# A wait of GpSimd between groups of gathers, moved from ahead of a group's second gather to ahead of its last

## What is computed

```python
e = jnp.stack([tbl_0[ids[:, 0]], tbl_1[ids[:, 1]], ..., tbl_25[ids[:, 25]]], axis=1)    # 512 x 26 x 128
combined = jnp.concatenate([dense[:, None, :], e], axis=1)                             # 512 x 27 x 128
interactions = jnp.einsum('bfd,bgd->bfg', combined, combined)
iu, ju = jnp.triu_indices(27, k=1)
z = jnp.concatenate([dense, interactions[:, iu, ju]], axis=1)
h = jnp.concatenate([z, dense], axis=1)                                                # 512 x 607
h = jnp.maximum(h @ W_top1 + b_top1, 0.0)                                              # 607 -> 512
h = jnp.maximum(h @ W_top2 + b_top2, 0.0)                                              # 512 -> 256
y = h @ W_top3                                                                         # 256 -> 1
```

## Time and profile before

| | us |
|---|---|
| median of 3 runs (145.75 to 149.02) | 146.39 |
| the profiled execution | 147.18 |
| its span, first to last instruction | 145.4 |
| POOL busy / PE busy in the span | 80.0 / 103.3 |
| ACT busy / DVE busy | 72.3 / 75.0 |
| mean granted TensorE clock (share of full) | 0.881 |

### The profile page before, as it was taken

How to read it: one execution, slowest core, us unless ns; L and a number is a source line. 1 busy time by engine, 2 the same in 40 slices (tenths; PEclk the granted TensorE clock), 3 DMA queues, 4 the chain that set the end, 5 groups by cost and what they waited for, 6 DMA issues and landing times.

```text
span 145.4 us, 2762 instructions
## 1 busy us (share of the span) xinstructions
PE 103.3 (71%) x1052; PEld 93.8 (65%) x1052; DVE 75.0 (52%) x181; ACT 72.3 (50%) x179; POOL 80.0 (55%) x89
## 2 busy tenths in 40 slices
PE   0677659990349961899399974989939493694993
PEld 0366458980139950887399963979929392592992
DVE  3499993579200628289068008960662993057000
ACT  6798494821112999635169632041694232158111
POOL 2677644627556677685667776776777675000000
PEclk9999955599556999789999999599999999689599
DMA  4844798562822211121211221221121122000000
GB/s 164 230 125 117 196 305 251 134 180 70 316 71 58 54 43 54 52 52 41 52 43 54 60 60 36 59 54 52 43 54 54 42 53 56 2 5 0 0 0 1
DMA packets 6291, 11.96 MB, mean 82 GB/s; under 512 B 2683, under 2 KB 3295, under 8 KB 6150
## 3 DMA queue, kind: packets, MB, share of 16 engines
q0 software_dynamic: 2624, 5.38, 14.0%
q1 hardware_dynamic: 3509, 6.15, 13.9%
q10 hardware_dynamic: 144, 0.26, 0.5%
HBM read 10.65 MB, written 0.00 MB: 73 GB/s over the span
## 4 chain that ended last, share of the span: by engine, by line
DMA 46%; POOL 27%; issue 13%; PE 9%; DVE 3%; ACT 1%; POOLq 0%
DMA rows<-in_tbl_dram,ids_i 44%; POOL rows L419 27%; PE ps L740 4%; DVE z L586 3%; PE ps L702 2%; DMA ids_i<-in_ids_dram 2%; PE ps L752 1%; PE ps L647 1%; DVE z L587 0%; PE ps L762 0%; PE ps L681 0%; ACT emb_t L485 0%; ACT y L521 0%; DVE h_t L614 0%; POOLq L206 0%
## 5 line engine op out<-in xcount | busy, mean ns | idle before, releaser
L419 POOL DMA_INDIRECT rows<-in_tbl_dram,ids_i x82 | 79.2, 966 | 41.7 <-DMA rows<-in_tbl_dram,ids_i 21.0
L552 DVE TENSOR_SCALAR hot<-ps,row_no 125x256 fp32r<-125x256 f32 x73 | 29.8, 475 | 18.3 <-PE ps L634 18.2
L494 ACT COPY z<-ps 32x80 f32<-32x80 f32 (+2 forms) x80 | 25.8, 323 | 13.8 <-PE ps L702 12.9
L664 PE MATMUL ps<-hot,tab_hi 125*128 125x256 f32 x88 | 27.7, 340 | 4.4 <-ACT emb_t L464 4.3
L681 PE MATMUL ps<-ident,rows 128*128 128x128 f32 x82 | 15.1, 304 | 21.2 <-DMA rows<-in_tbl_dram,ids_i 17.7
L667 PE MATMUL ps<-hot,tab_lo 125*128 125x256 f32 x88 | 26.7, 329 | 1.7 <-DVE tab_lo L540 1.7
L681 PEld LDWEIGHTS ps<-ident,rows 128*128 128x128 f32 x82 | 9.8, 152 | 24.3 <-DMA rows<-in_tbl_dram,ids_i 19.7
L485 ACT COPY emb_t<-ps 128x512 f32<-128x512 f32 (+2 forms) x22 | 12.7, 579 | 24.7 <-PE ps L681 24.5
L664 PEld LDWEIGHTS ps<-hot,tab_hi 125*128 125x128 f32 x88 | 20.7, 235 | 5.4 <-ACT emb_t L464 4.8
L667 PEld LDWEIGHTS ps<-hot,tab_lo 125*128 125x128 f32 x88 | 20.8, 236 | 2.2 <-DVE tab_lo L540 2.2
L586 DVE COPY z<-ps 32x80 f32<-32x80 f32 (+2 forms) x42 | 13.1, 313 | 14.5 <-PE ps L702 13.9
(11 more groups left out here) (48 smaller groups left out, 92.2 us busy)
## 6 DMA issues: line engine op xcount, KB each, us to landing
tab<-in_tbl_dram SPq DMA_DIRECT2D x6, 448.0 KB
rows<-in_tbl_dram,ids_i POOLq DMA_INDIRECT x82, 2.5
w_fold<-w_pair SPq DMA_DIRECT2D x1, 1024.0 KB
w<-in_W_top_dram SPq DMA_DIRECT2D x1, 512.0 KB, 6.8
tab<-in_tbl_dram SPq DMA_DIRECT2D x6, 52.0 KB
x_rows<-in_r_dense_features_dram ACTq DMA_DIRECT2D x1, 256.0 KB, 2.9
w_x<-in_W_top_dram SPq DMA_DIRECT2D x1, 256.0 KB, 4.2
h_t<-in_W_top_dram SPq DMA_DIRECT2D x1, 256.0 KB, 4.7
```

The source lines that it names most:

```text
L419: pool.indirect_dma_start(out=rows[:, t % 2, gathered.index(f), :], out_offset=None, in_=tables[f - 1], in_offset=bass.IndirectOffsetOnAxi ...
L494: last = nc.scalar.copy(dst, src)
L552: nc.vector.tensor_scalar(hot[0:RP, k % OHB], ps[0:RP, IDV[h] + n % 2, 0:HB], row_no[0:RP, c:c + 1], None, ALU.is_equal).then_inc(hot_dve, 1)
L664: nc.tensor.matmul(bank, tab_hi[0:RP, n, c], one_hot, start=c == 0, stop=False)
```

## The change

The wait keeps its condition and its semaphore. Only the gather ahead of which it stands is another: no longer the second (n = 1) but the last of the group (n = len(fetched) - 1).

```diff
                     for n, f in enumerate(fetched):
-                        if n == 1 and g:
+                        if n == len(fetched) - 1 and g:
                             pool.wait_ge(rows_in[t][g - 1], 16 * sum(a > 0 for a in features(groups_of(t)[g - 1])))
-                        elif n == 1 and t:
+                        elif n == len(fetched) - 1 and t:
                             pool.wait_ge(rows_in[t - 1][NG - 1], 16 * len(features(groups_of(t - 1)[NG - 1])))
                         pool.indirect_dma_start(
```

## The result

The changed kernel takes 141.01 us in the median of 4 runs (140.90 to 141.15), the kernel before 147.17 (145.75 to 149.02): 0.965 of it, 95% interval 0.962 to 0.969. The ratios leave out runs more than 1.5% above the fastest of their kernel, so 0.965 stands for 5.1 us and the two medians lie 6.2 apart. On another chip the ratio was 0.963 (0.958 to 0.968). The forecast was 140.8. The profiled execution took 141.03 us and its span 139.1, against 147.18 and 145.4.

A forecast was written before the change was run, and what follows sets the result against it. The prediction took POOL's issue of 82 gathers, held back by waits for landings, as the bound. Gains of 2.0 us early and 3.6 steady, 5.6 in all, took 146.39 to 140.8 us; range 136.5 to 143.8.

The forecast's parts named there:

- Steady part: From 49.1 us on: 13 moved waits are hidden, each leaving only POOL's pause; gain 3.6 us.
- The cover: From 49.1 us on: extra gathers issued meanwhile hide the landing, 3.2 us at longest against 3.75; failing, gain 0.
- case 5: Rival: waits from 49.1 us on cost nothing beyond the landing, only the earlier stretch gains; 144.4 us, chance 0.02.
- Early part: Up to 49.1 us: gathers issued earlier gain 2.0 us, low bound 1.6, high bound 7.0.
- Step two: Tile 0, group 4: the awaited gather lands at 31.5 as before; the group's last goes at 31.8, before 34.28.
- case 2: Rival: landings follow issues before 49.1 us too, gain there up to 7.0; 135.5 to 139 us, chance 0.13.
- Step three: Tile 0, group 5: the awaited gather takes 4.0 us, landing at 35.8; the second gather goes at 36.1, before 37.04.
- Step four: Tile 1, group 0: the awaited gather lands at 40.5 under the copy; the third goes at 40.8, gain 1.7 us.
- PE follows: Tiles 1 to 3: PE keeps up; the gather still decides at tile 3's group 5, by 3.5 us.
- Tail: From 123.94 us to the end: 21.5 us without gathers, unchanged.
- the forecast's own sign: At the kernel's end: a tail not 21.5 us long would show the forecast wrong.
- Slower, by gathers that take turns from the loads: Rival: extra gathers in flight at 20 to 24 us delay tables and weights; about 149.1 us or more, chance 0.04.

The follow-up runs named there:

- the first pair: Profiled executions of the kernel before and the changed kernel, from the main measurement: 147.18 and 141.03 us, spans 145.4 and 139.1.
- the second: Traces of the same two kernels run again without edit: medians 147.11 us before and 141.49 us changed, ratio 0.963.

## Why the prediction was right, point by point

**What bounds the kernel:** right. The gathers set the end, and still do.

**Steady part, forecast 3.6 us, measured 4.2** in the first pair and 5.3 in the second. All 13 moved waits are hidden: between 50 and 122 only four are left, those of group 5 in tiles 1 to 3 and one that costs 0.30, which is the pause. Idle time accounts for 3.9 of the 4.2, and gathers on which POOL itself was busy for longer than 0.94 (1.07, 1.19 and 1.41 before, 1.07 and 1.36 after) for 0.3. The 1.40 at 68.09 became 0.54, and another group 5 got 1.19: these vary from trace to trace, as the forecast left open. The cover held, with little to spare in groups of three: the longest landing was 3.5 against 3.75. (The forecast took 3.2 for the longest before; the chain has one of 3.34, issued at 64.49, still under 3.75.)

By the estimate of 2.15 us to landing from the Trainium skill (DMA: Bandwidth & Descriptors, Anatomy of one DMA) nothing would have been left to gain here. The traces had 2.5 and the gain came, so case 5 was rightly small.

**Early part, forecast 2.0 us, measured 0.9 in the first pair, 1.9 between the means.** That 2.0 and 1.9 agree is luck. The forecast put the start of the steady part at 47.1 (49.1 less 2.0), and all three traces with the new place have it at 48.2 to 48.5, over 1 us later. The mean comes out right because before starts it at 50.2 on average, while the forecast had only the trace with 49.1. Two steps were wrong, and they cancelled in part. Step two said that the gather of 23.5 would land at 31.5 as before, since the queue decides; it landed at 29.4, after 5.94, near its time of before. Group 4's last gather then went at 29.69 and not at 31.8, which the forecast had called the sign of case 2; case 2 did not come, since the next landing was late. Step three gave that one 4.0 us; it took 6.88 and landed at 36.6, so tile 0's last gather went at 36.82 in place of 36.1. With `w_pair` in pieces the first of these landings hardly changes (5.69) and the second falls to 3.13. So they are not one queue at an even 2.07 us a gather; the second hangs on how `w_pair` is loaded, and why is argued above. Step four was nearly as foreseen, 4.91 under the copy where 4.4 was taken. Tile 1's third gather went at 41.99 in place of 40.8.

**PE follows:** right in kind, and up to 1.2 us late. Forecast against measured for the gram of tiles 1, 2, 3: 69.4, 96.5, and 119.6 (118.3 and the 1.3 from landing to gram) against the timeline of PE in the changed kernel:

```profile
43.34 3.29 PE L702 MATMUL ps<-emb_t 128*64 128x52 f32 x64 [0.87 <-ACT emb_t L485]
...
70.65 3.94 PE L702 MATMUL ps<-emb_t 128*64 128x52 f32 x128 [0.77 <-ACT emb_t L485]
...
97.02 3.94 PE L702 MATMUL ps<-emb_t 128*64 128x52 f32 x128
...
119.11 0.44 PE L681 MATMUL ps<-ident,rows 128*128 128x128 f32 x2 [1.78 <-DMA rows<-in_tbl_dram,ids_i]
120.51 5.49 PE L702 MATMUL ps<-emb_t 128*64 128x52 f32 x128 [0.97 <-ACT emb_t L485]
```

Tile 0's gram half was to start 0.5 us earlier than 42.64 and started 0.7 later, as its last gather landed at 41.73 and not at 41.03; that is the 1.2 by which tile 1's gram is late. PE no longer waits for the gathers of tile 1's group 5, as said; for tile 3's it does, by 1.78 and 1.13 for the group before, where 3.5 was forecast.

**Tail, forecast unchanged:** no effect of the change shows, but it is 18.9 to 21.8 us from execution to execution, where the forecast took 21.5 as a constant. In the first pair it was 1.5 shorter. By the forecast's own sign that is wrong, and it made up for the early part in that pair's total.

**Slower, by gathers that take turns from the loads:** at most small. The copy's issue moved from 35.70 to 36.76 us in the first pair and from 36.06 to 36.79 in the second, 1.1 and 0.7 late, and tile 0's group 5, which lands beside it, was 0.7 late in the first. PE's one-hot products of tile 0 ended where they did.

**The total:** 140.8 against 141.01. The forecast took 5.6 from 146.39; measured were 6.2 from 147.17. The last gather, which was to go 5.6 us earlier, went 5.1 earlier in the first pair and 6.1 in the second. The mechanism is confirmed, and that the total came within 0.2 us is in part luck.

## To carry to other kernels

A wait that throttles a queue of transfers is worth its place in steps: with a step of 1.25 us and 2.5 to landing it was free from the third step on, and leaving it out altogether cost nothing, since another wait guards the row buffers. Ahead of moving waits in a stretch that is full, look at how the other loads there are cut: four loads in other pieces brought 2.5 to 3 us, more than the early waits. And a single pair of traces can misjudge a term by half of it (0.9 for 1.9 here), so take several traces of both kernels.

## What had not been expected of the hardware

- Two chips ran every version tried there at 203 to 215 us, where other chips had 133 to 152. PE, ACT and DVE stood still or nearly so in long stretches in which POOL issued gathers.
- With the old place of the wait the time scattered by 3.3 and 5.5 us, with the new one by 0.25 and 0.7 beside it. The start of the steady part (49.1 to 51.8 against 48.2 to 48.5) fits that, but was not tested apart, and the kernel with the new place and the pieces scattered by 3.6.
- How four loads were cut decided when all of `w_pair` was complete: 3.9 us between 25, 23, 19 and 17 rows whole and the same as 16 and a rest.
